# First-half expert results summed by gathers that add in SBUF, in place of sums on VectorE

## The reference

```python
xn = layernorm(x)
out = x + attn_branch(xn) + ffn_branch(xn)

# attn_branch: rmsnorm -> linear recurrence over the sequence (64 states) -> y
#   x1 = xn + y + D_skip * u ;  x1 + w2 @ (silu(w1 @ z) * (w3 @ z)),  z = rmsnorm(x1), 688 inner columns
# ffn_branch: 32 experts (256 -> 128 -> 256), each token goes to 8 of them
combine = routing weights, zero but for the 8 chosen experts of a token
g = silu(einsum('th,eih->tei', h, w_gate)); u = einsum('th,eih->tei', h, w_up)
routed = einsum('tei,ehi->th', g * u * combine[:, :, None], w_down)
shared = silu(h @ sh_gate.T) * (h @ sh_up.T) @ sh_down.T      # 256 inner columns
out += routed + shared
```

## Time and profile before

| | |
|---|---|
| median of 3 runs | 1974.25 us (1972.17 to 1979.03) |
| profiled execution | 1973.12 us |
| span of its trace | 1971.2 us |
| busy share PE / DVE / POOL / ACT | 92% / 53% / 53% / 33% |
| first gather of the first half starts | 1055.8 us |
| first gather of the second half starts | 1590.9 us |

### The profile page before, as it was taken

The page is one execution under the profiler, slowest core; times in us unless marked ns, Lnnn a source line. Parts: engine busy times, 40 slices in busy tenths (PEclk is TensorE's granted clock), DMA queues, the critical chain, the costliest instruction groups (busy, mean ns, idle before and its releaser), DMA issues.

```text
span 1971.2 us, 31040 instructions
## 1 busy us (share of the span) xinstructions
PE 1804.0 (92%) x9958; PEld 1346.9 (68%) x9960; DVE 1038.4 (53%) x2462; ACT 652.8 (33%) x1349; POOL 1050.9 (53%) x1057
## 2 busy tenths in 40 slices
PE   6798998999989999999999898888898869999995
PEld 3455555655568888889888787777787845555553
DVE  6587456333234555445455565566565635555554
ACT  5620222222224444444444343334343322222220
POOL 0003777777777777720004644445444157777666
PEclk9898999999989999999999999999999979999998
DMA  6804334563668889875557877777777653333333
GB/s 207 257 10 144 136 127 167 186 231 140 241 219 282 280 282 283 276 215 174 170 176 221 262 237 227 235 233 233 221 233 223 187 156 113 107 109 100 101 96 104
DMA packets 261671, 374.55 MB, mean 190 GB/s; under 512 B 30357, under 2 KB 227081, under 8 KB 260617
## 3 DMA queue, kind: packets, MB, share of 16 engines
q1 hardware_dynamic: 211448, 227.51, 37.5%
q0 software_dynamic: 49920, 145.03, 22.3%
q10 hardware_dynamic: 144, 0.03, 0.0%
HBM read 189.47 MB, written 182.98 MB: 189 GB/s over the span
## 4 chain that ended last, share of the span: by engine, by line
PE 66%; DMA 15%; DVE 12%; issue 3%; SPq 2%; ACT 1%; DVEq 1%; POOL 1%; POOLq 0%; ACTq 0%
PE ps L1155 21%; DMA arena<-sorted_rows 14%; PE ps L1239 14%; PE ps L1172 11%; PE ps L1253 9%; PE ps L1228 5%; DVE arena L1026 2%; DVE xe L940 2%; PE ps L1141 1%; PE ps L1112 1%; PE ps L1079 1%; PE ps L1128 1%; SPq L437 1%; DVE xe L941 1%; DMA big<-in_x 1%
## 5 line engine op out<-in xcount | busy, mean ns | idle before, releaser
L511 POOL DMA_INDIRECT xe<-results,slots x512 | 528.2, 1032 | 580.2 <-DMA results<-arena 252.1
L1239 PE MATMUL ps<-arena 128*128 128x128 f32 x4608 | 589.4, 281 | 41.9 <-DVE arena L1009 40.5
L1239 PEld LDWEIGHTS ps<-arena 128*128 128x128 f32 x4608 | 539.9, 193 | 111.1 <-ACT arena L634 60.6
L1155 PE MATMUL ps<-arena,w 128*128 128x512 f32 (+1 forms) x768 | 345.8, 593 | 0.0
L500 POOL DMA_INDIRECT sorted_rows<-big,slots x256 | 258.4, 1010 | 83.8 <-issue 77.7
L1253 PE MATMUL ps<-big,arena 128*128 x1152 | 297.7, 381 | 0.3 <-DVE arena L1017 0.3
L500 POOL DMA_INDIRECT sorted_rows<-xe,slots x256 | 252.9, 988 | 78.0 <-issue 78.0
L925 DVE TENSOR_TENSOR arena<-arena,ps 128x512 f32<-128x512 f32 (+1 forms) x128 | 87.8, 686 | 356.0 <-ACT arena L602 355.0
L602 ACT ACTIVATE arena<-ps 128x512 f32<-128x512 f32 (+1 forms) x128 | 76.3, 596 | 574.3 <-PE ps L1155 573.4
L1009 DVE COPY arena<-big 128x512 f32 x576 | 230.2, 441 | 64.4 <-issue 64.1
L639 ACT ACTIVATE arena<-ps 128x256 f32<-128x256 f32 x288 | 110.4, 383 | 423.2 <-PE ps L1239 423.2
(11 more groups left out here) (156 smaller groups left out, 1162.0 us busy)
## 6 DMA issues: line engine op xcount, KB each, us to landing
arena<-sorted_rows SPq DMA_DIRECT2D x288, 288.0 KB, 3.8
results<-arena SPq DMA_DIRECT2D x288, 256.0 KB, 2.6
big<-in_x SPq DMA_DIRECT2D x32, 512.0 KB, 4.3
sorted_rows<-big SPq DMA_DIRECT2D x2, 4608.0 KB, 23.9
xe<-results,slots POOLq DMA_INDIRECT x512, 3.2
out<-xe SPq DMA_DIRECT2D x64, 128.0 KB, 2.0
sorted_rows<-big SPq DMA_DIRECT2D x48, 144.0 KB, 1.8
big<-in_wexp SPq DMA_DIRECT2D x1, 5632.0 KB, 18.6
```

Source lines behind the costliest of these rows:

```text
L511: pool.indirect_dma_start(out=gathered_at[i % RING][:, k, :], out_offset=None, in_=results[half], in_offset=bass.IndirectOffsetOnAxis(ap=s ...
L1155: last = mm(ps[0:m, 2 + 2 * (s % 2) + u, :], w[:, u, c, lo:lo + m], src[:, c, :], start=c == 0, stop=c == DC - 1)
L1239: last = mm(ps[:, 2 + n % 2, (2 * s + u) * P:(2 * s + u + 1) * P], wgu[n % 2][:, s, at_w:at_w + INNER], rT[n % 2][:, (2 * s + c) * P:(2 * ...
```

## The change

The first half's 8 rows are no longer gathered side by side and added on DVE. POOL loads a whole group's parts (4 tiles, 512 KB) from `parts` into an accumulator in SBUF, then gathers choice after choice into the same place with `compute_op=ALU.add`, so that each gather adds its rows to what is there. The order is choice outside, tile inside: a gather waits until the gather of the choice before has landed on the same tile. POOL itself then stores the finished group to `out`. All of this is in POOL's own queue; DVE and SP have no part in it. The second half is left as it was, on DVE; its gathers now begin behind the last store of first-half sums, and SP waits for these stores too before it loads the parts of tiles 32 to 35.

```diff
+        acc = [xe[:, j * GT * D:(j + 1) * GT * D].rearrange("p (t d) -> p t d", d=D) for j in range(RING)]
...
-        def combine_after(n):
-
-            return [i for i in range(HT) if PAIRS + 6 + i * 13 // 3 == n]
...
             def load_part(i):
-                if i >= RING:
-                    sp.wait_ge(summed, i - RING + 1)
                 sp.dma_start(part_tile[i % RING], parts[i * P:(i + 1) * P, :]).then_inc(part_loaded[i % RING], 16)
...
                 if n + RING < ALL:
                     load_rows(n + RING)
-                for i in combine_after(n + 6):
-                    load_part(i)
-                for i in combine_after(n - 2):
-                    store_out(i)
...
             for g in range(FIRST, FIRST + 4):
                 load_x(g, g)
+            for j in range(RING):
+                sp.wait_ge(sums_stored[j], 16 * (HT // GT // RING))
             for i in range(HT, HT + GT):
                 load_part(i)
...
-            for half in range(HALVES):
-                results_stored(pool, PAIRS * (half + 1))
-                for i in range(half * HT, (half + 1) * HT):
-                    if i >= RING:
-                        pool.wait_ge(out_stored[i % RING], 16 * (i // RING))
-                    for k in range(K):
+            def load_acc(g):
+                if g >= RING:
+                    pool.wait_ge(sums_stored[g % RING], 16 * (g // RING))
+                pool.dma_start(acc[g % RING], group_rows(parts, g)).then_inc(acc_loaded[g % RING], 16)
+
+            def gather_sums(g):
+                pool.wait_ge(acc_loaded[g % RING], 16 * (g // RING + 1))
+                for k in range(K):
+                    for t in range(GT):
+                        if k:
+                            pool.wait_ge(added[g % RING][t], 16 * (K * (g // RING) + k))
                         pool.indirect_dma_start(
-                            out=gathered_at[i % RING][:, k, :], out_offset=None, in_=results[half],
-                            in_offset=bass.IndirectOffsetOnAxis(ap=slots[:, i, k:k + 1], axis=0)
-                        ).then_inc(gathered[i % RING], 16)
+                            out=acc[g % RING][:, t, :], out_offset=None, in_=results[0],
+                            in_offset=bass.IndirectOffsetOnAxis(ap=slots[:, g * GT + t, k:k + 1], axis=0),
+                            compute_op=ALU.add).then_inc(added[g % RING][t], 16)
+
+            def store_sums(g):
+                for t in range(GT):
+                    pool.wait_ge(added[g % RING][t], 16 * K * (g // RING + 1))
+                pool.dma_start(group_rows(out, g), acc[g % RING]).then_inc(sums_stored[g % RING], 16)
+
+            for par in range(2):
+                pool.wait_ge(part_stored[par], 16 * len(range(par, FIRST, 2)))
+            for g in range(RING):
+                load_acc(g)
+            results_stored(pool, PAIRS)
+            for g in range(HT // GT):
+                gather_sums(g)
+                if g >= 1:
+                    store_sums(g - 1)
+                if g >= 2 and g + 2 < HT // GT:
+                    load_acc(g + 2)
+            store_sums(HT // GT - 1)
+            for j in range(RING):
+                pool.wait_ge(sums_stored[j], 16 * (HT // GT // RING))
+            results_stored(pool, ALL)
+            for i in range(HT, NT):
...
                 if n >= 1:
                     e_out(n - 1)
-                for i in combine_after(n):
-                    combine(i)
```

More of the change, by code:

```diff
@@ L277, in build @@
         gathered = sems("gathered", RING)
+        added = [sems(f"added{j}_", GT) for j in range(RING)]
+        acc_loaded = sems("acc_loaded", RING)
+        sums_stored = sems("sums_stored", RING)
         part_loaded = sems("part_loaded", RING)
@@ L417, in load_part @@
             def load_part(i):
-                if i >= RING:
-                    sp.wait_ge(summed, i - RING + 1)
                 sp.dma_start(part_tile[i % RING], parts[i * P:(i + 1) * P, :]).then_inc(part_loaded[i % RING], 16)
             def store_out(i):
-                sp.wait_ge(summed, i + 1)
+                sp.wait_ge(summed, i - HT + 1)
                 sp.dma_start(out[i * P:(i + 1) * P, :], gathered_at[i % RING][:, 0, :]).then_inc(out_stored[i % RING], 16)
@@ L441, in _ @@
                     load_rows(n + RING)
-                for i in combine_after(n + 6):
-                    load_part(i)
-                for i in combine_after(n - 2):
-                    store_out(i)
-            assert not combine_after(ALL - 2) and not combine_after(ALL - 1)
             sp.wait_ge(wgu_ready, ALL)
@@ L461, in _ @@
             for q in range(RING):
-                sp.wait_ge(out_stored[q], 16 * (NT // RING))
+                sp.wait_ge(out_stored[q], 16 * (HT // RING))
         @block.gpsimd
@@ new lines, in _ @@
+            store_sums(HT // GT - 1)
[3 more added lines that the diff above has]
+            for i in range(HT, NT):
+                if i >= HT + RING:
+                    pool.wait_ge(out_stored[i % RING], 16 * (i // RING - HT // RING))
+                for k in range(K):
+                    pool.indirect_dma_start(
+                        out=gathered_at[i % RING][:, k, :], out_offset=None, in_=results[1],
+                        in_offset=bass.IndirectOffsetOnAxis(ap=slots[:, i, k:k + 1], axis=0)
+                    ).then_inc(gathered[i % RING], 16)
@@ L938, in combine @@
                 y = gathered_at[i % RING]
-                dve.wait_ge(gathered[i % RING], 16 * K * (i // RING + 1))
+                dve.wait_ge(gathered[i % RING], 16 * K * ((i - HT) // RING + 1))
                 do(tt(y[:, 0:4, :], y[:, 0:4, :], y[:, 4:8, :], ALU.add))
@@ L945, in combine @@
                 else:
-                    dve.wait_ge(part_loaded[i % RING], 16 * (i // RING + 1))
+                    dve.wait_ge(part_loaded[i % RING], 16)
                     rest = part_tile[i % RING]
```

## The result

The changed kernel takes 1992.32 us (median of 4 runs, 1991.51 to 1996.98) against 1973.21 for the kernel before (4 runs). The ratio is 1.0094, 95% interval 1.0067 to 1.0121: slower, where 1953 us and faster had been forecast, and 6 us outside the range.

What follows compares the result with a forecast made beforehand. DVE's sums and late row loads bound the expert stage beside gathers; 98 pairs at 3.70 us while gathers run (362 us) and 46 at 3.26 (150) make 512 against 532, 20 us won: 1953 from 1973.1, range 1920 to 1986.

Steps and rivals of the forecast that it cites:

- What bounds the stretch: Expert stage beside first-half gathers: DVE's sums, about 1.2 us each, 39 us at most, and late loads of sorted rows.
- The lap of the row load: Expert stage: one lap from row load to next serves two pairs, so a pair costs at least (landing + 2.68) / 2.
- The DMA engines: Beside adding gathers: an add takes 1.5 times a plain gather's engine time; share 0.54, landing 4.6, pair 3.70 us.
- the upper end: DMA engines: an add takes twice a plain gather's engine time; share 0.72, row load landing 5.1, pair 3.96 us.
- the case of that rule: Rival on the DMA engines: adding doubles engine time, pair 3.96 us, 3 us lost, 1976 us, or 1984; chance 0.20.
- the doubled end: DMA engines, add at twice a plain gather's time: share 0.72, landing 5.1, pair 3.96 us, 1976 us; chance 0.20.
- the lower end: DMA engines: an add costs what a plain gather does; landing 4.05, pair 3.44 us, 1930 us; rival's chance 0.25.
- POOL's time: POOL's queue: gathers each 1.295 us, 332 us, plus 30 for plain DMAs, 362 in all; longer adds hidden either way.
- A rival at 1976 to 1984: DMA engines: adding doubles engine time; pair 3.96 us gives 1976, landing 5.1, or 1984 at pair 4.1; chance 0.20.
- POOL's plain DMAs: POOL's queue: 12 loads and stores of 512 KB take 30 us; the same bytes as SP's 128 KB ones, so nothing else.
- The chain of adds: First-half gathers: each waits for one four issues earlier, 5.2 us; covered unless adding makes landings 40% longer.
- the late second half: Rival: first-half gathers end late, delaying the second half's; decides from 8.1 us a round, 2028 us at 9; chance 0.13.

Runs made afterwards that it cites:

- e6: Kernel before, each first-half sum's four steps spread behind four successive pairs on DVE, and SP issuing row loads ahead of stores: 1917.33 us, ratio 0.9711.
- e4: Kernel before, three of the four steps of each first-half sum left out on DVE, gathers, loads and stores kept: 1945.18 us, ratio 0.9853.
- f1: Changed kernel, POOL's 512 KB loads of parts and stores of sums cut into 128 KB pieces: 1981.69 us, ratio 1.0050 to the kernel before.
- f2: f1 with first-half gathers writing over and not adding, so first-half sums left out: 1948.06 us, ratio 0.9863 to the kernel before.
- g1: f2 with a POOL memset behind each gather, to pace gathers about like adding ones: 1945.60 us, ratio 0.9854 to the kernel before.
- e2: Changed kernel, SP issuing the row load of pair n+4 ahead of the store of pair n: 1945.41 us, ratio 0.9845 to the kernel before.
- e1: Changed kernel, first-half gathers writing over the accumulator and not adding, so first-half sums left out: 1958.05 us, ratio 0.9910 to the kernel before.
- f3: Changed kernel with f1's 128 KB pieces on POOL and e2's row loads ahead of stores on SP: 1931.41 us, ratio 0.9782 to the kernel before.

## Why the prediction was wrong

Two terms of the sum failed: the price of a pair while gathers run (3.70 forecast, 3.90 measured) and the length of that stretch (362 forecast, 491 measured). With only the price at its upper end, 3.96, the sum loses 3 us; with only the length at 491, 133 pairs and 11 at 3.26 make 527 and it still wins 5; with both, 124 pairs and 20 at 3.26 make 556 against 532, 24 us lost. Measured were 546, 14 us lost there.

*What bounds the stretch: right.* Sums and row loads, and they add up (e6). The sums were worth 32 us in e4, where 39 at most was said.

*The lap of the row load: right*, and the most useful step. (Landing + 2.68) / 2 + 0.07 met f1, f2 and g1 within 0.03 us, and e2 acted on it alone. It is a floor: with a step of each sum left on DVE it gives 3.36 for e4 (3.52 measured), and with the bursts 3.86 for the changed kernel (3.98). PE's own pace is a little below the 3.26 read off the quiet stretch: with e2's order 47 pairs pass there in place of 46.

*The DMA engines: the engine time was mis-sized, and the upper end came near by luck.* I took 1.5 times a plain gather's engine time; it is 1.85 (f1 against g1). The Trainium skill (Collectives: The Full Stack, section "The bandwidth ceiling: the fold count and why AG ≠ RS ≠ AR"), speaking of the reduce step of a collective, says that its add needs two source reads and so runs at half the rate of a copy. The trace nearly agrees, with 1.85 times the time, and the case of that rule, which I gave 0.20, was a better guide than a middle that no row supported. But the doubled end's landing of 5.1 and pair of 3.96 lie near the measured 4.9 and 3.98 by two errors against each other: its share was 0.72, at one gather each 1.3 us, and POOL at one each 1.9 us kept it to 0.49 to 0.51; and I took the landing's slope from the scatters, 2.9 us for a full share, where gathers make it (4.4 - 3.0) / 0.38 = 3.7 (f2), (4.9 - 3.0) / 0.49 = 3.9 (f1) and (4.2 - 3.0) / 0.28 = 4.3 (g1). That slope is also why the lower end was off: plain gathers back to back make 4.4, not 4.05. And about 0.1 of the 3.98 is the bursts' (f1: 3.87).

*POOL's time: this is the step that took the time out of the range.* I put a longer adding gather at nothing, "hidden either way", because the first half would still be done before the second half's results. That cover holds: POOL waits 50 us there. But the stretch's length was also a factor of the sum, 362 us at the price of a pair beside gathers, and there I left it at its lower end. The adding gather takes 1.58 us on POOL, a little over the upper bound that I had worked out (0.995 + 0.555), so the stretch is 491 us. A rival at 1976 to 1984 had nearly the right price for a pair and the wrong number of pairs; with 491 us its price makes 1997.

*POOL's plain DMAs: put at 30 us of POOL's time and none of anyone else's.* The four 512 KB store-and-load pairs are each followed by a row load of 6.6 to 8.5 us and a stretch at the halved clock, and the first four loads hold the pairs at 861 to 946 us. Cutting all of them up wins 9 to 11 us (after against f1, e1 against f2). In the traces of f1 more of that lies at the first loads than beside the gathers (7 and 3 us), in those of e1 and f2 less (5 and 14). I said "the same bytes"; the size of each mattered.

*The chain of adds, the late second half: right that they cost nothing in this kernel.* 3.0 us of waits, and a 50 us margin. The margin is there because the pairs are slow: it is 13.8 us in e2, and gone in f3 and g1.

What each step is worth can be read from these kernels (profiled executions, us; the columns are set by ACT's once-a-pair line):

| kernel | pairs 0 to 144 | pairs 144 to 287 | behind pair 287 |
|---|---|---|---|
| before | 479 | 532 | 384 |
| e4: no folds on DVE | 479 | 500 | 384 |
| g1: no sums, POOL at the adding pace, pieces | 481 | 496 | 390 |
| f1: the same pace, adding, pieces | 478 | 543 | 383 |
| after: adding, 512 KB transfers | 485 | 546 | 383 |

In pairs 144 to 287, taking the sums off DVE wins 32 to 36 us, adding costs 47, and bursts cost 3 beside adding gathers; the first loads cost 6 to 7 more ahead of them. In ratios the steps are -1.5% (e4), 0.0% (g1 against e4), +2.0% (f1 against g1) and +0.4% (after against f1). That they add up to the measured +0.9% proves nothing: each is the difference of two neighbouring kernels of this table, so they must. And the 2.0% for adding is too low by what g1 loses at the start of stage 4.

Not settled: of the 1.85, how much is the second read and how much the smaller packets; no run separates these. One row bears on it: in g1 SP's queue, with packets of 1.02 KB, holds the engines 0.516 x 240 x 16 / 38.31 = 52 us for each MB, POOL's plain gathers, with 2.7 KB, 58, and adding gathers and pieces in f1 99. So packets of 1 KB need not be dear, which speaks for the second read; but that is another queue and other transfers.

## What to carry to other kernels

Where a cost is price times length, carry the bounds of both: work that is hidden from the next stage may still lengthen a stretch in which everything else is dearer. Cover that comes from another stage's slowness goes when that stage gets faster (f3, g1). A sum that moves into the DMA engines isn't free just because they work on their own; beside a stage that already uses half of them it lands on the transfer with the shortest lead. And before moving work between engines, look at the order on the queue and at how much of it stands at once: two such edits (e6) were worth 56 us, where the sums that the change took off DVE were worth 32.

## What the runs showed of the hardware

- An adding gather of 128 rows of 1 KB takes 14.2 us of DMA engine time where a plain one takes 7.65, and 1.58 us of POOL where a plain one takes 1.00.
- Gathers delay another queue's loads more than scatters do at the same share of the engines: the row load lands at 4.2 with POOL's gathers (and pieces) at 0.281 in g1, and at 3.9 with its scatters at 0.309 in the kernel before.
- Beside adding gathers the record of a plain 128 KB DMA on POOL is 1.26 us long (f1: 17.6 us for 14), beside plain ones 0.59 (g1: 8.8 us for 15). But it begins while the gather before it still runs: of f1's 240 us, 188.1 are gathers and 36.2 the gaps before them, which leaves 0.63 for each of the 25 pieces.
